# A gated cross-attention block with routed experts on one core: the experts' first product with its weights resident and the tokens streamed by pair

## The reference

```python
x = x + tanh(g_xattn) * cross_attention(layernorm(x), ctx)        # 32 query heads, 8 key/value heads
x = x + tanh(g_ffn) * ffn(layernorm(x))

# ffn: 64 experts of rank 16, 16 of them per token
scores = xf @ Wr.T                               # 64 router scores per token
top_vals, top_idx = top_k(scores, 16)
G = scatter(softmax(top_vals), top_idx)          # gates, zero outside the 16
h = einsum('nd,krd->nkr', xf, A)                 # 64 * 16 = 1024 ranks per token: "first product"
out = einsum('nkr,kdr->nd', h * G[:, :, None], B) * 2   # "second product"
```

## Time and profile before

| | us |
|---|---|
| median of 3 runs (lowest, highest) | 2451.65 (2449.57, 2452.21) |
| the profiled execution | 2446.73 |
| its span, first to last instruction | 2444.7 |
| PE busy in the span | 2291.7 (94%) |
| stage A, from the first-product copy of entry 82 to that of entry 92 (B's first) | 2036.04 to 2280.30 |
| granted TensorE clock, mean | 0.975 of 2.4 GHz |

### The profile page before, as it was taken

One profiled execution on the slowest core, in us unless ns is written; L12 is line 12 of the kernel. 1 busy time (PEld: TensorE's weight loads), 2 busy tenths in 40 slices (PEclk: granted clock), 3 DMA queues, 4 the chain that ended last, 5 costly groups with the idle time before them and its releaser, 6 DMA issues.

```text
span 2444.7 us, 35172 instructions
## 1 busy us (share of the span) xinstructions
PE 2291.7 (94%) x11384; PEld 1914.1 (78%) x11384; DVE 1664.2 (68%) x2631; ACT 1174.5 (48%) x3731; POOL 1342.1 (55%) x1816
## 2 busy tenths in 40 slices
PE   5998999999999999999998799899999997878799
PEld 4777887888888878888887688687887885767587
DVE  6457558777777787777777555757558877464755
ACT  4446555666666766666667422324224334242321
POOL 5577668555666566665555245655556765424421
PEclk8999999999999999999999899999999999989899
DMA  4867546555555735652226256456455675656653
GB/s 165 251 186 266 179 160 245 169 142 173 143 175 147 257 112 141 179 150 92 87 94 200 93 176 210 145 170 224 138 171 185 210 266 214 179 191 170 233 175 133
DMA packets 213893, 427.63 MB, mean 175 GB/s; under 512 B 12496, under 2 KB 95696, under 8 KB 199120
## 3 DMA queue, kind: packets, MB, share of 16 engines
q1 hardware_dynamic: 210352, 400.21, 49.2%
q0 software_dynamic: 3360, 25.17, 5.4%
HBM read 301.07 MB, written 174.59 MB: 195 GB/s over the span
## 4 chain that ended last, share of the span: by engine, by line
PE 73%; DMA 7%; POOL 7%; DVE 6%; issue 4%; ACT 2%; SPq 1%; ACTq 0%; POOLq 0%; DVEq 0%
PE bank L749 20%; PE bank L751 20%; PE bank L750 20%; PE bank L807 4%; PE bank L815 2%; PE bank L795 2%; DMA x2t<-x_columns 2%; DVE t_lo L1250 2%; DVE s_lo L1250 2%; DMA staged<-in_w_a 1%; DMA staged<-in_ctx 1%; PE bank L832 1%; PE bank L831 1%; PE bank L830 1%; DMA gates_of_ranks<-gates_t 1%
## 5 line engine op out<-in xcount | busy, mean ns | idle before, releaser
L749 PE MATMUL bank<-t_hi,s_hi 128*128 128x512 f32 x2720 | 1109.7, 408 | 113.9 <-DVE s_lo L1250 43.7
L751 PE MATMUL bank<-t_hi,s_lo 128*128 128x512 f32 x2720 | 1077.4, 396 | 0.0
L750 PE MATMUL bank<-t_lo,s_hi 128*128 128x512 f32 x2720 | 1075.7, 395 | 0.0
L749 PEld LDWEIGHTS bank<-t_hi,s_hi 128*128 128x128 f32 x2720 | 520.1, 191 | 230.0 <-issue 85.6
L1250 DVE TENSOR_TENSOR s_lo<-staged,s_hi 128x512 fp32r<-128x512 f32 x676 | 562.5, 875 | 146.1 <-ACT s_hi L983 136.0
L751 PEld LDWEIGHTS bank<-t_hi,s_lo 128*128 128x128 f32 x2720 | 519.5, 191 | 114.6
L750 PEld LDWEIGHTS bank<-t_lo,s_hi 128*128 128x128 f32 x2720 | 521.1, 192 | 94.4
L983 ACT CAST s_hi<-staged 128x512 fp32r<-128x512 f32 x452 | 260.1, 622 | 427.0 <-DMA staged<-heads 188.6
L1698 POOL TENSOR_TENSOR staged<-staged 128x512 f32<-128x512 f32 x96 | 136.6, 1423 | 328.4 <-DMA staged<-gated 104.7
L1683 POOL TENSOR_SCALAR small<-small 128x4 f32<-128x4 f32 (+1 forms) x192 | 70.3, 366 | 408.3 <-ACT small L1069 332.1
L1250 DVE TENSOR_TENSOR t_lo<-t_raw,t_hi 128x2048 fp32r<-128x2048 f32 x77 | 200.9, 2616 | 36.2 <-ACT t_hi L974 27.4
(11 more groups left out here) (122 smaller groups left out, 2877.7 us busy)
## 6 DMA issues: line engine op xcount, KB each, us to landing
heads<-heads SPq DMA_DIRECT2D x128, 256.0 KB, 3.1
combos<-in_sets SPq DMA_DIRECT2D x12, 2048.0 KB, 13.2
t_raw<-combos SPq DMA_DIRECT2D x24, 1024.0 KB, 8.8
staged<-in_w_q SPq DMA_DIRECT2D x32, 768.0 KB, 5.3
staged<-heads SPq DMA_DIRECT2D x32, 768.0 KB, 5.9
t_raw<-in_sets SPq DMA_DIRECT2D x22, 1024.0 KB, 8.4
sums<-sums SPq DMA_DIRECT2D x18, 1024.0 KB, 8.0
sums<-sums SPq DMA_DIRECT2D x36, 512.0 KB, 4.7
```

Source lines behind the costliest of these rows:

```text
L749: nc.tensor.matmul(out, s_hi[w][:, cols], high, start=start, stop=False, skip_group_check=True)
L750: nc.tensor.matmul(out, s_hi[w][:, cols], low, start=False, stop=False, skip_group_check=True)
L751: done = nc.tensor.matmul(out, s_lo[w][:, cols], high, start=False, stop=at == 3, skip_group_check=True)
```

## The change

Stage A is turned round. The **weights A are the moving set** (set 8, resident for the whole stage) and the normalised tokens are streamed, one pair of sequences per entry: eight entries, 82 to 89; stage B is 90 to 97. What follows from it in the code:

- one moving set fewer (`TAUS` 11 to 10); set 8 has its sums made like the others, so the query entries carry 24 accumulation steps instead of 20 (up to the 28th query entry instead of the 24th);
- `x2_columns` keeps 4 blocks instead of 7: DVE's and POOL's sums of it (L1427 to L1432, L1768, L1770) go, ACT copies one block more, and DRAM gets 1 MB per pair instead of 1.75 MB; the pairs are taken in the order in which `finish` ends them;
- the router runs in each entry behind k = 3, on staged tiles that are there anyway: 24 matmuls of 128 x 256, with router weights split once beforehand (a load, one pass each on POOL, ACT and DVE, beside entries 59 to 62);
- `choose` handles the two token tiles of the pair, in four parts at beats 5, 6, and 0, 1 of the next entry;
- ranks lie along the row now, tokens on partitions. POOL multiplies by gates read with a step of zero over the 16 ranks, so nothing of the gates goes to DRAM;
- for stage B the gated ranks are transposed on PE (16 transposes per pair), copied by ACT, and written with one DMA of 1 MB.

```diff
-KV0, QA0, DRAIN0, O0, A0, B0, ENTRIES = 0, 16, 48, 50, 82, 92, 100
+KV0, QA0, DRAIN0, O0, A0, B0, ENTRIES = 0, 16, 48, 50, 82, 90, 98
...
-        self.t_order[8] = self.t_order[9] = (0, 2, 4, 5, 1, 3, 6)
...
+    GATED_AT = {2: (0, 1), 4: (2,), 5: (3,)}
+    COLUMNS_AT = {4: (0, 1), 6: (2,), 7: (3,)}
+    COPIED_AT = {5: (0, 1), 7: (2,), 8: (3,)}
+    OUT_AT = {9: (0,)}
...
-        return [(2 + u // 4, u % 4) for u, n in enumerate(n for n in range(2, 24) if n not in (15, 16)) if e == QA0 + n]
+        return [(2 + u // 4, u % 4) for u, n in enumerate(n for n in range(2, 28) if n not in (15, 16)) if e == QA0 + n]
...
     def pair_of_output(i):
-        return (i + 4) % 8
+        return 7 - i
...
             elif e < B0:
-                src = d.w_a[(e - A0) % 5 - 1]
+                i = e - A0
+                sp.wait_ge(ft_out, 16 * (i + 1))
+                src = d.x2t[pair_of_output(i)]
             else:
                 i = e - B0
-                for w in range(8):
-                    sp.wait_ge(h_out[w], 32 * (i // 4 + 1))
-                src = d.gated[pair_of_output(i)].rearrange("p b h q -> p b (h q)")
+                sp.wait_ge(h_out, 16 * (i + 1))
+                src = d.gated[pair_of_output(i)]
...
         def gated_out(beat):
...
+            for i, t in tiles_at(beat, OUT_AT):
+                sp.wait_ge(hc_copied, 4 * i + 4)
+                sp.dma_start(d.gated[pair_of_output(i)], gc[:, :, :]).then_inc(h_out, 16)
...
+        def router(i):
+
+            out = bank[score_banks(i)[0]][:, 0:2 * S].rearrange("p (b q) -> p b q", b=2)
+            pe.wait_ge(s_lo_done, plan.fill[A0 + i, 6])
...
+            for half in range(2):
+                for at in range(4):
+                    cols = slice(at * P, at * P + P)
+                    high, low = (s[:, 4 * half:4 * half + 3:2, cols] for s in (s_hi_all, s_lo_all))
+                    nc.tensor.matmul(out, rw_hi[:, half, at, :], high, start=half == 0 and at == 0, stop=False)
+                    nc.tensor.matmul(out, rw_hi[:, half, at, :], low, start=False, stop=False)
+                    done = nc.tensor.matmul(out, rw_lo[:, half, at, :], high, start=False, stop=half == 1 and at == 3)
+            done.then_inc(rt_done, 1)
...
+        def rank_columns(beat):
+            for i, t in tiles_at(beat, COLUMNS_AT):
+                n = 4 * i + t
+                pe.wait_ge(h_gated, n + 1)
...
+                for c in range(4):
+                    done = nc.tensor.transpose(bank[6 + t % 2][:, c * P:c * P + P], ring[4 * (i % 2) + t][:, c * P:c * P + P], ident[:, :])
+                done.then_inc(hc_done, 1)
...
         for e in range(A0, B0):
...
+            for j in SEVEN:
+                product(e, j)
                 finish(plan.beat0[e] + j)
-                if idx == 2 and j == 0:
-                    gate_columns(s)
+                rank_columns(plan.beat0[e] + j)
+                if j == 3:
+                    router(e - A0)
+                if j == 4:
+                    score_rows(e - A0)
...
         def gate(beat):
...
+            for i, t in tiles_at(beat, GATED_AT):
+                e, w, k = A0 + i, 4 * (i % 2) + t, (3, 4, 5, 6)[t]
...
                 pool.wait_ge(taken[BANK_OF[k]], plan.after[e, k])
...
+                pool.wait_ge(gate_step, GATE_STEPS * (i + 1))
+                tile = ring[w][:, :].rearrange("p (e r) -> p e r", r=RANK)
+                gates = w1[i % 2][:, rows, 32 * half:32 * half + 32].unsqueeze(2).to_broadcast([P, 32, RANK])
+                nc.gpsimd.tensor_tensor(tile, tile, gates, ALU.mult).then_inc(h_gated, 1)
```

More of the change, by code:

```diff
@@ L84, in __init__ @@
                 loads += 1
-                sums += 0 if entry.router else 4
+                sums += 4
                 if entry.tau not in self.first_of_set:
@@ L240, in program @@
     m = Sbuf(nc)
-    t_hi, t_lo, t_raw, s_hi, s_lo = [], [], [], [], []
+    t_hi, t_lo, t_raw = [], [], []
     for k in SEVEN:
@@ L734, in part @@
             if at == 0:
[L735 to L737 removed]
+                pe.wait_ge(s_lo_done, plan.fill[e, k])
+                if plan.first_of_set[entry.tau] == e:
                     pe.wait_ge(t_lo_done, plan.t_fill(entry.tau, k))
@@ L952, in before_next @@
         order, count = plan.a_order(plan.next(e)) if plan.next(e) else (), len(entries[e].ks)
-        if entries[plan.next(e) or 0].router:
-            return {count - 2: order[:1], count - 1: order[1:]}.get(j, ())
         return {count - 2: order[:2], count - 1: order[2:4]}.get(j, ())
     def after_start(e, j):
-        if e == 0 or entries[e].router:
+        if e == 0:
             return ()
@@ L988, in first_product @@
             if e:
-                k = 5 if entries[e - 1].router else 3
                 before = e - 1 if entries[e - 1].ks else e - 3
-                act.wait_ge(taken[BANK_OF[k]], plan.after[before, k])
+                act.wait_ge(taken[3], plan.after[before, 3])
                 if O0 <= before < A0:
@@ new lines, in router_exps, with rank_columns @@
+        def router_exps(i):
+            act.wait_ge(gate_max, i + 1)
+            for w in range(2):
+                done = nc.scalar.activation(ex[:, w, :], sc[:, w, :], ACT.Exp, bias=g_nmax[:, w:w + 1])
+            done.then_inc(gate_exp, 1)
+        def rank_columns(beat):
+            for i, t in tiles_at(beat, COPIED_AT):
+                n = 4 * i + t
+                act.wait_ge(hc_done, n + 1)
+                if i and t == 0:
+                    act.wait_ge(h_out, 16 * i)
+                nc.scalar.copy(gc[:, block_of(t), :], bank[6 + t % 2][:, :]).then_inc(hc_copied, 1)
@@ L1692, in sums @@
         def sums(e):
-            if e is None or entries[e].router:
+            if e is None:
                 return
```

465 lines of the change are left out of this document (191 added, 274 removed).

## The result

The changed kernel takes 2408.79 us (median of four runs, 2407.35 to 2409.32) against 2451.84 (2449.57 to 2452.21) before, run on the same chip: a ratio of 0.9821 with a 95% interval of 0.9809 to 0.9833. It is 43.05 us faster. 2411 was forecast, with a range of 2395 to 2431.

A forecast was written before the change was run, and what follows sets the result against it. Stage A was taken as limited by the gates' DRAM trip, SP's queue, crowded DMA engines and two token-set changes. 234.4 + 9.5 + 10.4 + 6.0 + 0.4 = 260.7 against 301.2 gave 2406.2, plus 4.9: 2411 us, range 2395 to 2431.

The forecast's parts named there:

- PE's work: PE's own time from entry 81 to 90 after the change: 234.4 us summed, 24.5 for entry 83.
- Steady chains: Stage A entries without a set change: two new chains end close to PE's need, 1.0 us an entry, 6.0 over six.
- chain (2): Staged load, four POOL sums, then rank tile 2's multiplication: ready at 22.5 us, PE needs it at 23.6, margin 1.1.
- chain (1): At beat 5 DVE's tile copy, search part and next entry's first `s_lo`: 2.7 to 3.8 us against PE's 3.2.
- First change of set: Entries 81 to 82, projection into stage A, bound by DVE: a stall of 9.5 us.
- Second change: Entries 89 to 90, into stage B: a stall of 10.4 us, with 4.5 for the last pair's search on DVE.
- The window: From the first-product copy of entry 81 to that of stage B's second entry; 301.2 us before the change.
- Outside the window: Everything before entry 81's copy and after stage B's second: little changes, +0.4 us for a last transpose group in stage B.
- Steady chains bind: Rival: staged load takes 9 us, not 5.9, so tile 2 is 2.0 us late in seven entries; 2425, chance 0.20.
- changes as dear as the one before: Rival: both set changes cost 20.1 us each, like the one behind the second half before; +18, 2429, chance 0.11.
- The slower one: Rival: staged load lands 8.3 us later, PE waits for POOL's tile 2, 7.2 us in each of eight entries; 2462, chance 0.04.
- The clock rival: Rival: with transpose groups among its matmuls, stage A runs at clock 0.83, 40 us more; 2451, chance 0.02.

## Why the prediction held, step by step

The total was right, 2.2 us above what was measured, in part by luck: the terms were off by more and went against each other.

- *What bounds it.* Right, and shown by runs. The gates' trip alone carries 35.3 of the 43.05 us, one change of set 7.8. The shares of its parts (SP's queue, the DMA crowd, POOL's wait) stay open.
- *PE's work.* Right: 24.42 measured for entry 83, 24.5 forecast; 23.97 for a full entry, 24.04 forecast.
- *Steady chains, 1.0 us an entry.* Wrong: it was 0, and PE is busy 120.00 of 120. In the five intervals that touch no change of set this is 5.3 us with the rounding. Two sizes were wrong, and most of both hangs on whether POOL and DVE meet. The 1.5 us of the earlier trace rows that I took for all five POOL passes of chain (2) is a mean. The same instruction's minimum and median before, and the new one over the whole kernel (ns min/median/max):

```profile
L1795 POOL TENSOR_TENSOR ranks<-ranks,gates_of_ranks x32: 1261/1290/3324, 2105.4 to 2287.5; 128x512 f32<-128x512 f32 x32
```

```profile
L1757 POOL TENSOR_TENSOR ranks<-ranks,gates_of_tokens x32: 1049/1066/3110, 2073.8 to 2264.7; 128x512 f32<-128x512 f32 x32
```

By their times in the trace, the 13 passes before that have no DVE pass beside them lie between 1261 and 1288; the 19 that have one take 1286 to 3324. In a steady entry after the change no DVE pass runs beside the four sums and they take 5.1 us, not 6.0; the multiplication takes 1.07, not 1.5, of which about 0.2 is its other operand. That is 1.3 of the 1.9 us by which the margin is wider than forecast. For chain (1) the first part of the search took 0.85 us where I had estimated 1.3, and I had left room for the 1.78 of the earlier trace rows. The low halves of the staged tile in 2093 to 2213 us:

```profile
L1224 DVE TENSOR_TENSOR s_lo<-staged,s_hi x35: 673/684/693, 2093.9 to 2210.8; 128x512 fp32r<-128x512 f32 x35
```

All 35 are short, though eight POOL passes per entry run in this stretch, because the two hardly meet: 30 have no POOL pass beside them, and the other 5 began before POOL's. Where they meet, the longer times are there. In the last 100 us of the projection (1900 to 2000, kernel after) 20 of the 35 `s_lo` have a POOL pass beside them and 14 of these take over 0.8 us, up to 1.78; none of the 15 others exceeds 0.694. Two lines of that stretch:

```profile
1903.03 4.91 DVE L1224 TENSOR_TENSOR s_lo<-staged,s_hi 128x512 fp32r<-128x512 f32 x3 [0.20 <-ACT s_hi L952]
1903.94 1.75 POOL L1665 TENSOR_TENSOR staged<-staged 128x512 f32<-128x512 f32 x1
```

So the prediction read the two values rightly, as DVE with and without a POOL pass beside it; what it didn't do was to lay the two engines' passes of a steady entry side by side.

- *First change of set.* 56.27 us less PE's own 44.9: a stall of 11.4, forecast 9.5. DVE is the busiest engine there, 50.20 of 58 us.
- *Second change.* 57.07 less 44.9: 12.2, forecast 10.4. The size is near, the composition wasn't: the search brings 1.9 to 3.3 rather than 4.5, and 2.96 is PE's wait for POOL's tile 2, behind four sums, which I had placed in the steady entries. The two overlap, as that wait falls to 1.3 without the search. The versions that multiply earlier gain 4 to 5 us here, so DVE isn't the only bound of that place. POOL and DVE do meet here: the 3110 ns multiplication is of this change, and one of the four sums takes 3.23 us instead of 1.29.
- *The window.* Forecast 260.3, measured 257.6: +1.9 in the first change, -0.1 in entry 83, -5.3 in the steady entries, +0.8 over the second change's two entries.
- *Outside the window.* I took +0.4, and it is 5.3 in the profiles: entry 81's copy comes 3.9 later than before, and the rest of stage B takes 1.4 more. The first is probably no cost of the change, but that isn't shown. The copy of entry 50 stands at 1379.81 us before and 1385.13 after, but at 1380.55 and 1386.09 in two versions of the kernel before, so the kernel before has it at either place. In the versions of the kernel after it was always late, between 1384.08 and 1387.18. The profiled execution before was 5.1 us below its median and that after 0.5; carrying the 4.9 of the former to the forecast was what made up for it, and that was luck. What moves that front part from run to run wasn't tried.
- *The accumulation steps, at nothing.* Right, by both runs.
- *The rivals.* "Steady chains bind" and "changes as dear as the one before" didn't happen. The slower one is a real mechanism of this kernel: with the loads held back PE stood in front of tile 2 as it said, and 39 us came back, though the gated write, held with them, would have cost nearly as much by itself. It didn't come about because the loads land in 5.9 us. Its price per entry came near (7.2 forecast, 7.3 to 9.0 measured) by two errors against each other: the margin was 3.0 and not 1.1, and the lower clock wasn't in it. Its threshold was wrongly added: 5.1 + 1.1 + 5.9 is 12.1, not 12.5. The clock rival is refuted at this dose and at three times it.

## What to carry to other kernels

Before using a row's mean as a price, look at its minimum and median, and at what ran beside the long ones: here a mean of 1.5 us stood for passes of 1.26 to 1.29 alone and up to 3.3 beside a DVE pass. Then lay the two engines' passes of one entry side by side: whether they meet decides which value holds. A transfer's lateness costs what is queued behind it and behind its consumers: before a load is called hidden or dear, write down what follows it on its queue and on the engine that reads it. And when an engine is full in a stretch, taking work from it gives only as much as the next chain is behind; moving multiplications ahead of four sums gave at least as much here (4.25 us, 4.0 in the profile) as taking out the whole search (1.9, 3.3 in the profile).

## What was not expected of the hardware

- A POOL multiplication of 128x512 in f32 whose second operand repeats along the rows took 1.07 us, a sum of two full tiles 1.27 to 1.30 in the same entries, both with no DVE pass of two tiles beside them.
- DVE's `s_lo` slows beside a POOL pass (up to 1.78 us from 0.68) and POOL's passes beside DVE's (up to 3.23 from 1.29), but in 120 us of steady entries, with POOL busy 47.54, no `s_lo` did: the passes hardly met, and five that met a multiplication had begun first (0.68), the multiplication beside them taking 1.38.
- The write of 1 MB takes 8.1 us at the median in the steady entries and 11.68 beside a refill.
- With the loads held back, PE was busy 82.38 of 100 us and the granted clock was 0.90; with 48 transposes an entry and no wait it was 1.00.
